# A decoder layer with attention and 64 experts on one core: attention pairs written out, a group's work on TensorE reordered, two weight remainders on VectorE, the Silu table loaded ahead of the expert loop

## What is computed

```python
x = x + attention(layernorm(x))        # 16 heads of 64, causal, rotary
x = x + cross(layernorm(x), ctx)       # softmax over keys
x = x + moe(layernorm(x))              # 64 experts, top 8, silu(gate) * up, F = 384
# attention, per head:
q, k, v = proj(Wq), proj(Wk), proj(Wv) # q and k rotated
out = softmax(mask(q @ k.T / 8)) @ v   # over 1024 keys, then @ Wo
```

## Time and profile before

| | |
|---|---|
| median of 3 runs | 7863.1 us (7861.7 to 7868.93) |
| profiled execution | 7857.78 us |
| its span | 7856.2 us |
| PE's last turn of probabilities in attention (L433) | starts at 2506.2 us |
| loop over the experts | begins at 3803 us, runs to the end |
| PE busy over the span | 7249.5 us (92%) |
| granted clock of PE, mean | 0.966 |

### The profile page before, as it was taken

One profiled execution on the slowest core, in us unless ns is written; L12 is line 12 of the kernel. 1 busy time (PEld: TensorE's weight loads), 2 busy tenths in 40 slices (PEclk: granted clock), 3 DMA queues, 4 the chain that ended last, 5 costly groups with the idle time before them and its releaser, 6 DMA issues.

```text
span 7856.2 us, 127734 instructions
## 1 busy us (share of the span) xinstructions
PE 7249.5 (92%) x39855; PEld 6147.3 (78%) x39856; DVE 4038.7 (51%) x8063; ACT 3578.2 (46%) x6728; POOL 1745.9 (22%) x1646
## 2 busy tenths in 40 slices
PE   8997997997996988986699999999999999999999
PEld 7887886886885777875588888888888888888887
DVE  6666666666665443345544444444444444444444
ACT  5665665665665221120244444444444444444444
POOL 1111111111110000000233333333333333333333
PEclk9998998998998999997799999999999999999999
DMA  1101111111112212121456555565555665555555
GB/s 58 34 25 47 30 33 43 34 30 42 29 33 66 70 65 81 62 67 41 114 161 163 158 157 159 158 180 156 158 159 156 162 180 158 158 160 157 160 158 147
DMA packets 286466, 826.59 MB, mean 105 GB/s; under 512 B 35873, under 2 KB 103457, under 8 KB 286113
## 3 DMA queue, kind: packets, MB, share of 16 engines
q0 software_dynamic: 98928, 365.58, 20.0%
q1 hardware_dynamic: 187184, 456.61, 17.2%
HBM read 615.37 MB, written 206.70 MB: 105 GB/s over the span
## 4 chain that ended last, share of the span: by engine, by line
PE 47%; issue 2%; DVE 1%; ACT 1%; ACTq 1%; POOL 0%; DMA 0%; DVEq 0%; POOLq 0%
PE ps_gu L1612 10%; PE ps_gu L1614 10%; PE ps_gu L1613 10%; PE ps_y L1612 4%; PE ps_y L1614 4%; PE ps_y L1613 4%; PE ps_xe L1632 3%; PE ps_xe L1641 1%; PE ps_l L1621 1%; ACTq L1482 1%; DVE gu_lo L1972 1%; ACT gu_hi L1793 1%; PE ps_h L1724 0%; DVE logits L1886 0%; ACT xtail_hi L1765 0%
## 5 line engine op out<-in xcount | busy, mean ns | idle before, releaser
L1612 PE MATMUL ps_gu<-xs_hi,gu_hi 128*128 128x512 f32 x3072 | 1223.1, 398 | 44.2 <-DVE gu_lo L1972 44.2
L1614 PE MATMUL ps_gu<-xs_hi,gu_lo 128*128 128x512 f32 x3072 | 1204.7, 392 | 0.0
L1613 PE MATMUL ps_gu<-xs_lo,gu_hi 128*128 128x512 f32 x3072 | 1200.6, 391 | 0.0
L347 PE MATMUL ps_qkv<-w_hi,xt_hi 128*128 128x384 f32 x1920 | 708.4, 369 | 52.1 <-DVE v L637 51.9
L1612 PEld LDWEIGHTS ps_gu<-xs_hi,gu_hi 128*128 128x128 f32 x3072 | 577.6, 188 | 188.4 <-DVE gu_lo L1972 72.0
L1591 POOL TENSOR_TENSOR dn_lo<-raw_w,dn_hi 128x512 fp32r<-128x512 f32 x384 | 484.9, 1299 | 912.9 <-ACT dn_hi L1793 912.9
L1614 PEld LDWEIGHTS ps_gu<-xs_hi,gu_lo 128*128 128x128 f32 x3072 | 577.2, 188 | 129.1
L1613 PEld LDWEIGHTS ps_gu<-xs_lo,gu_hi 128*128 128x128 f32 x3072 | 578.0, 188 | 120.2
L707 DVE TENSOR_TENSOR pt_lo<-ps_t,pt_hi 128x512 fp32r<-128x512 f32 (+3 forms) x768 | 425.4, 554 | 448.4 <-ACT pt_hi L556 435.8
L347 PE MATMUL ps_qkv<-w_hi,xt_lo 128*128 128x384 f32 x1920 | 650.5, 339 | 0.0
L347 PE MATMUL ps_qkv<-w_lo,xt_hi 128*128 128x384 f32 x1920 | 648.6, 338 | 0.0
(11 more groups left out here) (304 smaller groups left out, 16426.9 us busy)
## 6 DMA issues: line engine op xcount, KB each, us to landing
raw_w<-w_gu SPq DMA_DIRECT2D x384, 512.0 KB
raw_w<-w_down SPq DMA_DIRECT2D x192, 512.0 KB
w_raw<-wqkv SPq DMA_DIRECT2D x260, 192.0 KB, 2.6
out<-residual SPq DMA_DIRECT2D x36, 512.0 KB, 2.6
probs<-x SPq DMA_DIRECT2D x32, 512.0 KB, 3.4
attn_out<-out_t POOLq DMA_DIRECT2D x128, 128.0 KB, 2.2
residual<-x SPq DMA_DIRECT2D x32, 512.0 KB, 4.1
stage<-attn_out SPq DMA_DIRECT2D x32, 512.0 KB, 5.2
```

The costliest lines, as they stand in the source:

```text
L347: mm = pe.matmul(out, xs[:, k, a], ws[:, k, :], start=(n == 0), stop=(n == 3 * HB - 1))
L1612: pe.matmul(out, a_hi, w_hi, start=first, stop=False)
L1613: pe.matmul(out, a_hi, w_lo, start=False, stop=False)
L1614: return pe.matmul(out, a_lo, w_hi, start=False, stop=last)
```

## The change

In attention:
- pairs 1 to 6 are written out like the others; the loop over the batches stays;
- where place 1 of a group isn't the first step of a unit, PE turns that step's block ahead of the group's 12 matmuls, not after them (`turned_early`: groups 0, 2, 3, 4, 6, 7);
- in group 0, PE does the scores of step 2 after the 6 matmuls of the projection, not before, and DVE rotates before it takes that block's maximum;
- `w_lo` of blocks 5 and 7 is formed by DVE, at the ends of steps 0 and 1 (in the prologue, rounds 1 and 2); ACT splits block 6 right after `pt_hi` of step 1; whoever waits for `w_lo` waits for the semaphore of the engine that forms it.

In the experts the Silu on `warm` is done once, before the first split ahead of the loop, and no longer in each iteration.

```diff
-    W_OF_STEP = {..., 0: (1, (4, 5)), 1: (1, (6, 7))}
+    W_OF_STEP = {..., 0: (1, (4, 5)), 1: (1, (7,))}
+    POOL_K, DVE_K = (0, 1, 2, 3, 4, 6), (5, 7)
...
+        def wait_w_lo(eng, j, k):
+            if k in DVE_K:
+                eng.wait_ge(dve_lo_ok, START + j * len(DVE_K) + DVE_K.index(k) + 1)
+            else:
+                eng.wait_ge(pool_lo_ok, START + j * len(POOL_K) + POOL_K.index(k) + 1)
...
                 attention(j, 0, True, False)
-                with eng.Fori(0, (NP - 2) // 2) as two:
-                    attention(j + two * 2 + 1, 1, False, False)
-                    attention(j + two * 2 + 2, 0, False, False)
+                for pair in range(1, NP - 1):
+                    attention(j + pair, pair % 2, False, False)
                 attention(j + (NP - 1), 1, False, True)
... (PE)
+                def turned_early(s):
+                    return not last and s % PER == 1 and STEPS[s][1] > 0
+
+                for s, (u, kb) in enumerate(STEPS):
+                    group, place = divmod(s, PER)
+                    if not turned_early(s):
+                        turn_probs(s)
+                    late_scores = group == 0 and place == PER - 1 and not last
+                    if not late_scores:
+                        next_scores(s)
...
                         if place == 0:
+                            if turned_early(s + 1):
+                                turn_probs(s + 1)
                             pe.wait_ge(qkv_read, START + j * TB + TB + group)
                         qkv(j + 1, group, PARTS[place], ps_qkv[:, 0:W])
+                    if late_scores:
+                        next_scores(s)
                     if place == PER - 1:
                         weigh_values(...)
... (ACT, step s)
                     act.activation(pt_hi[...], ps_t[...], ACT.Copy).then_inc(tile_hi_ok, 1)
+                    if s == 1 and not last:
+                        split_w(j + 1, 6)
                     for args in fresh:
                         normalise(*args)
... (DVE, step s)
+                    late_scores = group == 0 and place == PER - 1 and not last
+                    if late_scores:
+                        rotate(j + 1, 1 - slot, group, ps_qkv, ...)
                     for ahead, unit, i in next_queries(s, last):
                         maxima(j + ahead, unit, i)
...
-                    if place == PER - 1 and not last:
+                    if place == PER - 1 and not last and not late_scores:
                         rotate(j + 1, 1 - slot, group, ps_qkv, ...)
...
+                    if s < len(DVE_K) and not last:
+                        rest_of_w(j + 1, DVE_K[s])
... (experts, ACT)
             act.wait_ge(set_up, START + 13)
+            act.activation(warm[:, :], warm[:, :], ACT.Silu)
             for i in range(SUP):
                 split_super(0, i)
...
                 finish_last(e + t0)
-                act.activation(warm[:, :], warm[:, :], ACT.Silu)
                 split(2)
```

More of the change, by code:

```diff
@@ L131, in self_attention @@
     SLOTS = 4
[L133 removed]
+    W_OF_STEP = {NS - 2: (2, (0, 1)), NS - 1: (2, (2, 3)), 0: (1, (4, 5)), 1: (1, (7,))}
+    POOL_K, DVE_K = (0, 1, 2, 3, 4, 6), (5, 7)
     XS = GQ
@@ L196, in self_attention @@
         xn_ok, xt_ok, xt_hi_ok, xt_lo_ok = (m.sem(n) for n in ("xn_ok", "xt_ok", "xt_hi_ok", "xt_lo_ok"))
-        w_hi_ok, w_lo_ok, w_early = m.sem("w_hi_ok"), m.sem("w_lo_ok"), m.sem("w_early")
+        w_hi_ok, pool_lo_ok, dve_lo_ok, w_early = (m.sem(n) for n in ("w_hi_ok", "pool_lo_ok", "dve_lo_ok", "w_early"))
         qkv_ok, qkv_read = m.sem("qkv_ok"), m.sem("qkv_read")
@@ L236, in first_w @@
                 for k in range(SLOTS):
-                    sp.wait_ge(w_lo_ok, START + (j - 1) * HB + k + SLOTS + 1)
+                    wait_w_lo(sp, j - 1, k + SLOTS)
                     load_w(pair, k)
@@ L242, in rest_of_w @@
                 for k in range(SLOTS, HB):
-                    sp.wait_ge(w_lo_ok, START + j * HB + k - SLOTS + 1)
+                    wait_w_lo(sp, j, k - SLOTS)
                     load_w(pair, k)
@@ L275, in rest_of_w @@
                 pool.wait_ge(w_hi_ok, START + j * HB + k + 1)
-                pool.tensor_tensor(w_lo[:, k, :], w_raw[:, k % SLOTS, :], raw(w_hi[:, k, :]), ALU.subtract).then_inc(w_lo_ok, 1)
+                pool.tensor_tensor(w_lo[:, k, :], w_raw[:, k % SLOTS, :], raw(w_hi[:, k, :]), ALU.subtract).then_inc(pool_lo_ok, 1)
             def find_rstd(b, t):
@@ L306, in _ @@
                 prologue(b, b * NP)
-                for k in range(SLOTS, HB):
+                for k in POOL_K[SLOTS:]:
                     rest_of_w(b * NP + 1, k)
@@ L342, in qkv @@
                     if t == 0 and term == 0:
-                        pe.wait_ge(w_lo_ok, START + j * HB + k + 1)
+                        wait_w_lo(pe, j, k)
                     a = slice(t * P, (t + 1) * P)
@@ L422, in attention, with turn_probs @@
                 tiles = tile_order(last)
-                for s, (u, kb) in enumerate(STEPS):
+                def turn_probs(s):
+                    u, kb = STEPS[s]
                     h, g = UNITS[u]
-                    group, place = divmod(s, PER)
                     if kb == 0:
@@ L434, in attention, with next_scores @@
                     mm.then_inc(tile_ok, 1)
+                def next_scores(s):
                     for ahead, unit, i in next_queries(s, last):
@@ L652, in rest_of_qk, with rest_of_w @@
                                   ALU.subtract).then_inc(tile_lo_ok, 1)
+            def rest_of_w(j, k):
+                dve.wait_ge(w_hi_ok, START + j * HB + k + 1)
+                dve.tensor_tensor(w_lo[:, k, :], w_raw[:, k % SLOTS, :], raw(w_hi[:, k, :]), ALU.subtract).then_inc(dve_lo_ok, 1)
             def maxima(j, u, i):
@@ L682, in prologue @@
                         rest_of_x(b, i - 1)
+                    if 1 <= i <= len(DVE_K):
+                        rest_of_w(j, DVE_K[i - 1])
                     if i >= 4:
@@ L708, in attention @@
                                       ALU.subtract).then_inc(tile_lo_ok, 1)
+                    late_scores = group == 0 and place == PER - 1 and not last
+                    if late_scores:
+                        rotate(j + 1, 1 - slot, group, ps_qkv, first_tile(j) + tiles["qk", group] + 1)
                     for ahead, unit, i in next_queries(s, last):
```

1 line of the change is left out of this document (removed).

## The result

| | before | after |
|---|---|---|
| median | 7861.9 us (7857.0 to 7868.9, 12 runs) | 7882.2 us (7876.1 to 7886.1, 12 runs) |
| profiled execution | 7857.8 us | 7876.9 us |
| PE busy | 7249.5 us | 7273.4 us |

The ratio of the medians is 1.0024, with a 95% interval from 1.0017 to 1.0032. The changed kernel is slower by 20 us, just beyond what a measurement tells from no change. The forecast was 7887 us, 24 above the median shown then. The sum came out, but four of its six terms missed by 10 to 16 us each, two up and two down, and they cancelled. That the time was met is in good part luck.

The account below looks back on a forecast made before the run. PE, busy for 92% of the span, was taken to bound the kernel. The terms -28 - 15 - 9 + 56 + 2 + 18 gave +24 us, so 7882 for the profiled execution and 7887 for the median, range 7845 to 7920.

Parts of the forecast that it names:

- late order, the chain: Group 0: rotation ahead of the maximum makes PE's step 4 2.0 us late in 28 pairs, 56 us lost.
- clock: PE behind step 4's stops: 12 half-clock stretches of 1.5 us in 28 stops of 2.3 us, 18 us lost.
- the eight differences of L707: DVE's pair times: eight pairs ending in a jump back take 28.0 us more than eight without; this goes.
- What is filled are waits like that of step 21: PE's waits for the bank: turning early fills two of 0.16 us a pair, 9 us gained in 28 pairs.
- ACT's splits are the same in number: Weights term: ACT's splits counted as unchanged in number; the whole term was 2 us lost, in the prologues.
- three of seven: PE's stops over 1.8 us at or behind jumps back: three of seven had a half-clock stretch; applied to 28 stops, 12 stretches.
- C: Rival at PE's step 4: the stops are there but the clock stays up, 7869 us; chance 0.18.
- D: Rival at PE's step 4: the clock falls in each pair, 28 stretches, 42 us lost, 7911 us; chance 0.12.
- B: Rival at step 4: division already done, as rotation starts 1.6 us earlier; both waits saved, 7783 us; chance 0.18.
- E: Rival in the experts: the loop keeps a table load at its head, without the 15 us gain, 7902 us; chance 0.04.

Follow-up runs that it names:

- both orders undone: Changed kernel with PE's scores of step 2 ahead of the projection and DVE's maximum ahead of the rotation again, as before the change: 7805.2 us (ratio to before 0.9920).
- the filled stop: Changed kernel with ten extra matmuls of 384 columns, read by nobody, ahead of PE's step 4 in 28 pairs: 7842.9 us (0.9974).
- on POOL, old order: Changed kernel with group 0's old order on PE and DVE, remainders of blocks 5 and 7 on POOL, block 6 split at its old place: 7793.2 us (0.9916).
- block 6 split late: Kernel with the old order of group 0, blocks 5 and 7 still on DVE, ACT's split of block 6 back behind the rotated block: 7794.9 us (0.9915).
- `split_v` ahead: Changed kernel with ACT's copy of v of group 0 ahead of the division of the block before at step 2: 7882.6 us (1.0026).
- only DVE's order kept: Changed kernel with PE's scores of step 2 back ahead of the projection, DVE still rotating ahead of the maximum: 7884.1 us (1.0024).
- the weights on POOL: Changed kernel, late order kept, with remainders of blocks 5 and 7 on POOL and block 6 split at its old place: 7869.7 us (1.0010).

## Why the prediction was right, and where it wasn't

| term of the sum | predicted | measured | by |
|---|---|---|---|
| pairs written out | -28 | -26 | written out alone |
| Silu | -15 | -14 | moved alone |
| turning early | -9 | -25 | taken out |
| late order, the chain | +56 | +42 | both orders undone, 28 x 1.51 |
| clock | +18 | +34 | 21 stretches x 1.6; the filled stop |
| weights | +2 | +12 | on POOL, old order |
| sum | +24 | +23 | the change: +20 |

The parts add up elsewhere too: 7862 less 26, 14 and 25 is 7797 us, and the kernel with the old order of group 0 and the old weights took 7793.

**Pairs written out** and **Silu** hold by their own steps: the eight differences of L707 are gone and straight code costs 1 us at most; DVE's registers and not the length of the load set what the load was worth.

**The chain** was right link by link. Rotation at 8.7 us into the pair by the prediction (168.1 - 1.62 - 157.75), 8.52 measured; maximum 10.3 and 10.06; PE's turn 14.3 (172.05 - 157.75) and 14.06. It is 1.8 us and not 2.0 against the turn of before. The 42 us of the table stand against a kernel whose turn already comes 0.25 us later than before, at 12.53, through ACT's early split; that part is booked under the weights.

**Turning early** failed at the step "What is filled are waits like that of step 21". The waits were sized rightly, 0.32 us a pair against 0.39, but the order of the kinds of matmuls, which I costed at nothing, is worth more than they are, 0.5 us a pair.

**Weights** failed at the step "ACT's splits are the same in number". They are, but one of them moved ahead of the copy that PE's scores wait for. I followed DVE's and POOL's lists and not the one that had only been reordered. The two remainders on DVE I called rightly: nothing in a pair, and some 2 us in the prologues. The medians, 7794.9 and 7793.2 us, can't tell that from nothing; in the profiled executions attention ends 3.1 us later with them.

**The clock** was right in kind and half its size. A stretch cost 1.6 us and not 1.5, and there were 21 in 28 pairs and not 12. The step that failed is carrying "three of seven" over: it came from stops of 1.85 to 2.73 us at the back edges, and stops of one length were followed by a stretch in 8, 21 and 27 of 28 pairs in three kernels. Between C (none) and D (all) the profile of before could not tell. The Trainium skill, "TensorE: Matmul & The Clock Gate", section "HAM oscillation — how this bites in real kernels", says that a wait that comes back puts the clock down each time; its waits are for DMAs and last 3 to 5 us. The runs agree only in part: with stops of 2.1 us all but one pair had a stretch in one kernel, and 20 of 28 had none in another.

**Rivals.** B falls: the division was in the way by 0.3 us, not by the 1.6 it would need. C falls by the 21 stretches, D by the other seven. E falls by the single load.

## What to carry to other kernels

A wait of PE that a reordering fills is only gone if the next thing PE needs is ready sooner as well; here a new wait and a longer second one took back more than the first had cost, and moving DVE's work to prevent that put 1.6 us of rotation into a chain with 0.4 us of slack. Before moving a step, follow every engine's list past it, ACT's included, to the next semaphore that somebody waits for. And a stop of PE of some 2 us that recurs should be priced twice, once for itself and once at half clock behind it. Here ten matmuls that nobody reads, put into each of 28 such stops, gave back 39 us.

## What the runs showed of the hardware that I had not expected

**A two-input subtraction on DVE beside one on POOL takes up to twice as long.** Blocks 4 (POOL) and 5, 7 (DVE) in the timeline of the changed kernel:

```profile
235.25 1.01 POOL L283 TENSOR_TENSOR w_lo<-w_raw,w_hi 128x384 fp32r<-128x384 f32 x1 [1.17 <-ACT w_hi L497]
...
235.62 1.06 DVE L683 TENSOR_TENSOR w_lo<-w_raw,w_hi 128x384 fp32r<-128x384 f32 x1
...
239.63 0.56 DVE L683 TENSOR_TENSOR w_lo<-w_raw,w_hi 128x384 fp32r<-128x384 f32 x1
```

Block 5 overlaps POOL's remainder and takes 1.06 us, block 7 has POOL quiet and takes 0.56; POOL's own is no longer there than alone (1.01). The last instruction of a rotation, with two SBUF inputs as well, shows the same at the end of a pair. It took 0.68 us alone and here, beside POOL, 1.08:

```profile
232.11 1.08 DVE L669 TENSOR_TENSOR rotated<-r_cos,r_sin 128x512 f32<-128x512 f32 x1
```

POOL's remainder beside it takes 1.48 us and not 1.01, in all 28 pairs, so either engine can pay. In the kernel with block 6 split late, block 7 runs beside POOL's block 6 and takes 0.90. The Trainium skill, "GPSIMD Engine Reference", section "1. Specifications", lists just this contention, with DVE instructions that have two SBUF inputs; these rows bear it out.

**Equal stops, unequal clocks.** Stops of 2.11 us were followed by a half-clock stretch in 27 pairs with `split_v` ahead, in 21 of the changed kernel and in 8 with only DVE's order kept. The mean granted clock puts all executions of the three in this order, not only the profiled ones: 0.959 to 0.960, 0.960 to 0.962, 0.963 to 0.964. The traces show a pattern. Where a stop is followed by a stretch, this begins between 0.2 us before and 1.4 us after PE starts again, in these three kernels and the one with the weights on POOL. And the place moves from pair to pair. In the changed kernel it begins some 14.9, 14.5 and 14.1 us into three pairs in a row, and the next pair has none; three of the four batches show the whole pattern. PE starts again at 14.06, so a further step of 0.4 us would be too early. Windows of L740 at these places in four pairs in a row:

```profile
953.93:957.34 3.41, 0.69 (x1) 0.50 0.00 0
...
1097.29:1100.70 3.41, 0.69 (x1) 0.50 0.00 0
1168.97:1172.38 3.41, 0.69 (x1) 1.00 0.00 0
```

With `split_v` ahead a pair with a stretch takes 71.8 us and not 72.1, the place moves by only 0.1 us from pair to pair, and a single pair is missed, one whose stop comes 2.1 us later than in the others. The stops being equal, it seems to be the length of a pair that decides how many pairs pay. No run changed that length alone, so this is read off the traces and not tested. The filled stop shows that without the stop there is no stretch.

**The same stretch costs 1.6 us or nothing**, by what follows it: behind the stop of step 4 PE is the bound and all of it counts; ahead of the stop, in the kernel with the weights on POOL, it costs 0.5 us at most.
